# Gate products of three routed layers: tile tokens as standing operand, in groups between the turnings

## The reference, cut to what matters

```python
# layer 1: top 2 of softmax logits; layer 2: every expert with sigmoid > 0.5; layer 3: the best sigmoid
h      = layer_norm(x) * gain + shift          # layer 1 only; layers 2 and 3 use the plain normed x
logits = h @ gate_w + gate_b                   # (2048, 256) @ (256, 8)
weights, chosen = route(logits)
y      = sum over chosen experts e of weights[e] * (act(h @ W1[e] + b1[e]) @ W2[e] + b2[e])
```

## Time and profile before

| what | value |
|---|---|
| median of 3 executions | 2148.92 us (2139.27 to 2152.86) |
| the profiled execution | 2146.7 us |
| its span in the trace | 2144.9 us |
| PE busy | 1993.9 us, 93% of the span |
| DVE / ACT / POOL busy | 1045.7 / 932.4 / 718.5 us |
| granted PE clock, mean | 0.975 of full |
| routing stages of m1, m2, m3 | about 912 to 940, 1282 to 1317, 1962 to 1985 us |

### The profile page before, as it was taken

How to read it: one execution, slowest core, us unless ns; L and a number is a source line. 1 busy time by engine, 2 the same in 40 slices (tenths; PEclk the granted TensorE clock), 3 DMA queues, 4 the chain that set the end, 5 groups by cost and what they waited for, 6 DMA issues and landing times. The chain is left out here.

```text
span 2144.9 us, 39790 instructions
## 1 busy us (share of the span) xinstructions
PE 1993.9 (93%) x12594; PEld 1462.5 (68%) x12598; DVE 1045.7 (49%) x2419; ACT 932.4 (43%) x1932; POOL 718.5 (33%) x814
## 2 busy tenths in 40 slices
PE   6899999888999999879999878999999999798998
PEld 5576656642232332469999767999999999466897
DVE  6885853667877776352232155222222222576221
ACT  2422652257777777423333332333333333264232
POOL 0123973410000000224333332434334333585432
PEclk9999999999999999999999988999999999899999
DMA  5003300053111112155222164422222221602711
GB/s 169 20 1 132 129 1 1 1 164 60 39 45 46 43 39 62 67 181 155 33 37 33 25 209 155 127 35 33 35 36 35 36 36 27 190 21 61 232 32 23
DMA packets 125501, 150.45 MB, mean 70 GB/s; under 512 B 28278, under 2 KB 105943, under 8 KB 125389
## 3 DMA queue, kind: packets, MB, share of 16 engines
q1 hardware_dynamic: 94477, 116.41, 17.2%
q0 software_dynamic: 24288, 31.81, 9.1%
q10 hardware_dynamic: 6624, 0.79, 0.3%
HBM read 113.33 MB, written 37.38 MB: 70 GB/s over the span
## 5 line engine op out<-in xcount | busy, mean ns | idle before, releaser
L2088 PE MATMUL banks<-m_rowsT,x_normT 128*128 128x128 f32 x4032 | 473.0, 276 | 4.3 <-DVE m_rowsT L2276 2.5
L2088 PEld LDWEIGHTS banks<-m_rowsT,x_normT 128*128 128x128 f32 x4032 | 463.6, 193 | 18.8 <-DVE m_rowsT L2276 1.7
L2097 PE MATMUL banks<-m_experts,m_hT 128*128 x2016 | 455.7, 379 | 0.0
L2097 PEld LDWEIGHTS banks<-m_experts,m_hT 128*128 128x128 f32 x2016 | 373.4, 190 | 45.8
L2327 ACT ACTIVATE m_hT<-banks,m_bias 128x128 f32<-128x128 f32 x848 | 241.7, 368 | 246.6 <-PE banks L2088 246.6
L2003 POOL DMA_INDIRECT scratch_acc<-m_y,m_row_ids x106 | 172.0, 1623 | 403.0 <-ACT m_y L2337 366.5
L2796 ACT ACTIVATE sh_pT<-banks 128x1024 f32<-128x1024 f32 x256 | 250.8, 1024 | 26.0 <-PE banks L2753 25.9
L2276 DVE COPY m_rowsT<-banks 128x256 f32<-128x256 f32 x88 | 37.4, 425 | 413.2 <-PE banks L2079 413.2
L2337 ACT ACTIVATE m_y<-banks,m_weight 128x256 f32<-128x256 f32 x126 | 59.6, 473 | 351.7 <-PE banks L2100 289.0
L2820 DVE TENSOR_REDUCE sh_mhalf<-banks 128x1 f32<-128x512 f32 x308 | 194.2, 684 | 35.2 <-PE banks L2701 35.2
L2260 DVE TENSOR_SCALAR x_normT<-m_experts 128x2048 f32 x129 | 167.8, 1301 | 74.6 <-issue 69.8
(11 more groups left out here) (411 smaller groups left out, 2777.3 us busy)
## 6 DMA issues: line engine op xcount, KB each, us to landing
m_experts<-L_W SPq DMA_DIRECT2D x32, 1024.0 KB, 11.0
m_experts<-L1f_W SPq DMA_DIRECT2D x16, 1024.0 KB, 9.1
a_bt<-bias SPq DMA_DIRECT2D x16, 616.0 KB, 3.8
scratch_parts<-sp_part SPq DMA_DIRECT2D x48, 128.0 KB, 1.9
scratch_rows<-x_norm SPq DMA_DIRECT2D x12, 512.0 KB, 3.4
sh_ks<-scratch_parts SPq DMA_DIRECT2D x93, 64.0 KB, 2.3
sh_qs<-scratch_parts SPq DMA_DIRECT2D x90, 64.0 KB, 2.3
scratch_acc<-x_resid SPq DMA_DIRECT2D x8, 512.0 KB, 2.9
```

The lines of the kernel that those rows point to most:

```text
L2088: mm = pe.matmul(ps[:, H_BANK[u] + f // 4, f % 4 * P:(f % 4 + 1) * P], w1_tile[:, u, k, f * P:(f + 1) * P], rowsT[:, u, k, :], start=(k == ...
L2097: mm = pe.matmul(ps[:, Y_BANK[u], 0:D], hT[:, u, f, :], experts.w2[:, bass.ds(slot_of(e), 1), f, :], start=(f == 0), stop=(f == FB - 1 and ...
```

## The change

The weights are no longer widened, the eight gate products of a layer become 32, and their operands change places. For each tile of 128 tokens and each half of the channels, the turned tile (128 tokens) is the standing operand and the 8 weight columns move. The result has tokens on partitions, so the copy of L2169 and the four transposes of L2048 are gone, and the bias is added straight from bank 0. The products are issued in groups of four tiles, between the turnings.

```diff
-        wg_sb, bg_sb, wide_gate = params["wg"], params["bg"], sb("wide_gate", [P, KD, 32])
+        wg_sb, bg_sb = params["wg"], params["bg"]
...
-            pool.memset(wide_gate[:], 0.0).then_inc(gate_wide, 1)
-            pool.wait_ge(gate_wide, 1)
-            params.wait(pool)
-            pool.tensor_copy(wide_gate[:, :, 0:EXPERTS], wg_sb[:]).then_inc(gate_wide, 1)
...
             core.keep_busy(pe, 7, 2)
-            for g in range(NCH):
+
+            def turn_tokens(g):
                 pe.wait_ge(tile_normed, 4 * g + 4)
                 for k in range(KD):
                     for j in range(4):
                         mm = pe.transpose(ps[:, 2 * g + k, j * P:(j + 1) * P], xn[:, 4 * g + j, k * P:(k + 1) * P], core.ident[:])
                     mm.then_inc(transposed, 1)
-            pe.wait_ge(gate_wide, 2)
-            for g in range(NCH):
+
+            def gate(g):
                 pe.wait_ge(evac_act, turns_before(g, False))
                 if turns_before(g, True):
                     pe.wait_ge(evac_dve, turns_before(g, True))
-                for k in range(KD):
-                    mm = pe.matmul(ps[32 * g:32 * (g + 1), GATE_BANK, :], wide_gate[:, k, :], xnT[:, k, g * CH:(g + 1) * CH],
-                                   start=(k == 0), stop=(k == KD - 1))
-            mm.then_inc(g_mm, 1)
-            pe.wait_ge(logits_sb, 1)
-            for j in range(4):
-                mm = pe.transpose(ps[:, TURNED_BANK, j * P:(j + 1) * P], turned[:, j * P:(j + 1) * P], core.ident[:])
-            mm.then_inc(logits_mm, 1)
+                for t in range(4 * g, 4 * g + 4):
+                    for k in range(KD):
+                        mm = pe.matmul(ps[:, GATE_BANK, t * EXPERTS:(t + 1) * EXPERTS], xnT[:, k, t * P:(t + 1) * P], wg_sb[:, k, :],
+                                       start=(k == 0), stop=(k == KD - 1))
+                return mm
+
+            turn_tokens(0)
+            turn_tokens(1)
+            params.wait(pe)
+            gate(0)
+            turn_tokens(2)
+            gate(1)
+            turn_tokens(3)
+            gate(2)
+            gate(3).then_inc(g_mm, 1)
             core.keep_busy(pe, SPARE_BANK, 6)
...
+            dve.wait_ge(made, 2)
             dve.wait_ge(g_mm, 1)
-            dve.tensor_copy(turned, ps[:, GATE_BANK, :]).then_inc(logits_sb, 1)
-            dve.wait_ge(made, 2)
-            dve.wait_ge(logits_mm, 1)
-            logits = ps[:, TURNED_BANK, :].rearrange("p (j g c) -> p g j c", j=4, c=32)[:, :, :, 0:EXPERTS]
-            link(dve.tensor_tensor(lg.rearrange("p (g j) e -> p g j e", j=4), logits,
-                                   bg_sb[:].unsqueeze(1).unsqueeze(1).broadcast_to([P, NCH, 4, EXPERTS]), ALU.add))
+            logits = ps[:, GATE_BANK, 0:NT * EXPERTS].rearrange("p (t e) -> p t e", e=EXPERTS)
+            link(dve.tensor_tensor(lg[:], logits, bg_sb[:].unsqueeze(1).broadcast_to([P, NT, EXPERTS]), ALU.add))
```

More of the change, by code:

```diff
@@ L1883, in routed_layer @@
         w1_tile = xnT[:].rearrange("p u (k f) -> p u k f", k=KD)
-        eps_done, rstd_done, tile_normed, gate_wide = sem("eps"), sem("rstd"), sem("normed"), sem("gate_wide")
+        eps_done, rstd_done, tile_normed = sem("eps"), sem("rstd"), sem("normed")
         transposed, evac_act, evac_dve = sem("transposed"), sem("evac_act"), sem("evac_dve")
         stored, made, x_in = sem("stored"), sem("made"), core.reloaded
-        logits_sb, logits_mm, wide, ends_known, pairs_done, where_mm, where_done = (
-            sem(n) for n in ("logits_sb", "logits_mm", "wide", "ends_known", "pairs", "where_mm", "where"))
+        wide, ends_known, pairs_done, where_mm, where_done = (
+            sem(n) for n in ("wide", "ends_known", "pairs", "where_mm", "where"))
         core.reloads += not last
@@ L1904, in routed_layer @@
         R_BANK, H_BANK, Y_BANK, RANK_BANK, TABLE_BANK = (0, 7), (1, 3), (5, 6), 5, 6
-        GATE_BANK, TURNED_BANK, WHERE_BANK, SPARE_BANK, COLUMN_AT = 0, 2, 7, 4, CH // 2
+        GATE_BANK, WHERE_BANK, SPARE_BANK, COLUMN_AT = 0, 7, 4, CH // 2
         DVE_TURNS = ((2, 1), (3, 1))
```

## The result

| | median us | executions |
|---|---|---|
| before | 2145.15 | 4 (2139.27 to 2152.86) |
| changed | 2171.51 | 4 (2163.69 to 2175.57) |

The ratio is 1.0109, with a 95% interval of 1.0082 to 1.0136: 18 to 29 us slower, 23 by the ratio itself and 26 by the medians. The forecast was 25.0 us slower. The two profiled executions (2146.7 and 2168.14) differ by 21.4.

What follows compares the result with a forecast made beforehand. PE was taken to bound the new gate stretch: 8.8 us of work net of the removal, 11.1 for the clock's fall in the gate and 5.1 for the fillers make 25.0 us, forecasting 2173.9 us, range 2153 to 2184.

Steps and rivals of the forecast that it cites:

- What bounds it: Three routing stages: a chain from gate through bias add to POOL's first gather; a stage ends later by the add's delay.
- What is removed: Between gate and bias add: copy, four transposes and two handovers go, 1.5 us a layer; one handover of 0.04 us stays.
- Weight loads at 0.116 us: New gate: 64 loads of 128 float32 columns a layer at 0.116 us each, 7.4 us of PE.
- No room between the turnings: Gate loads hardly hide between the turnings; adds come 2.4, 3.05 and 3.35 us later, together 8.8 us with the removal included.
- The clock falls in the gate: Granted clock halves after 3.7 us of gate products, doubling gate(2) and gate(3): 3.7 us more a layer, 11.1 in all.
- my outer bound: Gate: if the clock falls 3.7 us after the first product by wall clock, 16.6 replaces 11.1 us; sum 30.5 (2179.4).
- The fillers: Six filler products behind the gate take 5.0 instead of 2.76 us at the lower clock, adding 5.1 us over three layers.
- The sum: Whole kernel: 8.8 + 11.1 + 5.1 = 25.0 us slower, 2173.9 us against the median.
- The rival of the clock that holds: Gate and fillers stay at full clock, so only 8.8 us are lost: 2157.7 us; chance 0.31.
- The faster rival: Small float32 gate products take 0.041 us each, two thirds hidden between turnings; add 2.9 us sooner in m1, 2140.4; chance 0.05.
- No change: POOL's gather waits for something else and the stage hides 3 us: 2149 us; chance 0.04.

Runs made afterwards that it cites:

- doubled loads: The changed kernel with the 8 weight columns moved eight times over (64 columns) and each gate product issued twice: 2171.1 us, ratio 1.0112 to the kernel before.
- the 32-column run: The changed kernel with the gate's 8 weight columns moved four times over, 32 moving columns in each product: 2147.65 us, ratio 1.0012 to the kernel before.
- the second trace: The changed kernel timed and traced once more, with no edit: 2166.22 us, ratio 1.0075 to the kernel before.
- the runs that hold it: The changed kernel with the gate's 8 weight columns moved four or eight times over: 2147.65 us (ratio 1.0012) and 2151.7 us (1.0019) to the kernel before.

## Why the prediction was right, point by point

- **What bounds it.** Held inside the stages: the chain from gate to gather moved as one piece (6.6 us at the add and 6.6 at the gather in m1). That nothing else would move did not hold: the three stages are 24.8 us longer in the trace, the span 21.5, since the stretch from m2's first gather to m3 took 5.8 us less and the one ahead of m1 2.45 more. The prediction had put both at nothing.
- **What is removed.** Held: the add follows the gate by one handover (0.12 us, where 0.04 was predicted), PE being the one it waits for.
- **Weight loads at 0.116 us.** Nearly: 0.106 at full clock. The Trainium skill's columns divided by 1.2 ("TensorE: Matmul & The Clock Gate", section on LDWEIGHTS) gives 0.107, and the trace agrees at the full clock; at the lower one a load took 0.213. My row was read wrong: its 16 loads last 1.86 us with an overlap, but the next load starts 1.73 us behind the first (1248.01 to 1249.74), which is 0.108 each. Over 64 loads in three layers the 0.116 was 1.9 us too high.
- **No room between the turnings.** Held, by the doubled loads. With the clock held, the adds of the 32-column run come 2.0, 2.4 and 2.8 us later, 7.2 together, where 8.8 was predicted. The low clock at the turnings of m2 and m3 costs only in the changed order, where PE is the bound; in the order before it cost nothing in m2 and 0.4 us in m3.
- **The clock falls in the gate.** Held, and it decided the case: 11.1 us in the gate was predicted; from the adds, 6.65 + 7.40 + 7.44 = 21.5 less the 7.2 above are 14.3. The mis-sized step is when it falls. I let 3.7 us of gate products pass, turnings not counted, so that only gate(2) and gate(3) would be slow. In this trace it fell 3.3 to 3.8 us after the first gate product by the clock on the wall, in the middle of gate(1), which was near my outer bound. The turnings between did not put it off. In other executions of the same instructions it fell sooner, later or not at all, so no single moment could have been right.
- **The fillers.** Mis-sized: 5.1 us were predicted behind the adds, 24.8 - 21.5 = 3.3 measured. The six fillers took 4.71, 4.47 and 4.75 us, because the clock came back while they ran. The price of 5.0 was itself misread: in the earlier trace rows the 4.18 us belong to 9 records, so 12 at the lower clock are 5.6; in m2 of the second trace, where the clock stayed low to their end, they took 5.47.
- **The sum.** 8.8 + 11.1 + 5.1 = 25.0 was predicted, 7.2 + 14.3 + 3.3 = 24.8 measured. The mechanism is right, but that the sum fits so well is luck: errors of -1.6, +3.2 and -1.8 us cancel, and the second timing of the same kernel is 16 us slower than before instead of 23.
- **The rival of the clock that holds** was worth 8.8 us; the runs that hold it are 2.6 and 4.1 us slower than before. The Trainium skill's section on oscillation ("TensorE: Matmul & The Clock Gate") ties the fall to idle gaps; here it fell with PE and its loads at 1.00 in the rows, so by this case that is not the whole rule. **The faster rival** asked for 0.07 us a load; it is 0.106. **No change** is out: the gather moved with the add.

What stays open: what sets the moment of the fall, with the same instructions; whether weight loads count at all for the clock (no run changed their number alone at 8 columns); and the 5.8 us between m2 and m3. The last may explain in part why the runs that hold the clock, 2.6 and 4.1 us slower, lie below the sums of their first counts (7.2 and 8.4, just outside their intervals): they too took 642.1 us there, against 648.1 in the one trace of the kernel before.

## What to carry to other kernels

Swapping operands so that the small side moves turns a few long products into many that are bound by their weight load; count the loads, and ask whether PE has idle time for them where they land. Then look at the granted clock: a PE whose rows read busy 1.00 can still lose half its clock when the products are very short, and here the fall cost more than twice as much as the work (17.6 of the 24.8 us). Repeating the gate's moving operand 4 or 8 times cost nothing that shows and held the clock; the table's, which is strided, became slow by it, so measure a product first.

## What was not expected of the hardware

- The clock fell from 1.00 to 0.50 in an unbroken stream of 128x8 float32 products, with or without turnings between them, in ten of twelve gates, 2.9 to 4.6 us behind the first, and in one gate of the same stream it held.
- Products with every 16th f16 element moving took 1.9 ns a column (0.125 us for 64, 0.302 for 160), against 0.072 us for 16. The lower clock did not slow them: in m2, 25 of 64 columns started in 3 us at 1.00 and 27 at 0.50.
- Four gate groups of 32 standing columns (float32, 512 moving) took 2.94 us together, one alone 1.90, and two as long as four.
